# Early spread rows, states and y side by side, and one scan in place of two, in a Mamba-2 layer with a ternary feed-forward block

## The reference

```python
proj = rmsnorm(x) @ in_proj_w                  # z, x, B, C, dt: 2048+2048+512+512+32 columns
xBC  = silu(conv4(xBC) + conv_b)               # causal convolution of 4 taps, per channel
dt   = softplus(dt_raw + dt_bias); dA = exp(-dt * exp(A_log))
# per head (32 heads of 64 channels; 8 groups of B and C with 64 states each)
h_t  = dA_t * h_{t-1} + (dt_t * x_t) B_t^T     # 64 x 64 state
y_t  = h_t C_t + D * x_t
g    = y * silu(z);  g = g * rsqrt(mean(g^2 per group) + eps) * gate_norm_w
x    = x + (norm(x) + g @ out_proj_w)          # then the feed-forward block on the rows
```

## Time and profile before

| | |
|---|---|
| median of 3 runs | 1142.57 us (1141.39 to 1144.17) |
| the profiled execution: its own time, its span | 1145.73 us, 1143.9 us |
| DVE busy | 1059.9 us, 93% of the span |
| PE busy | 1033.2 us, 90% |
| ACT busy | 970.0 us, 85% |
| POOL busy | 868.6 us, 76% |
| granted PE clock, mean | 0.959 of full speed |
| from 260 to 860 us: idle of DVE in 120 us | about 1.1 us |
| DMA, mean | 20 GB/s |

### The profile page before, as it was taken

One profiled execution on the slowest core, in us unless ns is written; L12 is line 12 of the kernel. 1 busy time (PEld: TensorE's weight loads), 2 busy tenths in 40 slices (PEclk: granted clock), 3 DMA queues, 4 the chain that ended last, 5 costly groups with the idle time before them and its releaser, 6 DMA issues.

```text
span 1143.9 us, 26227 instructions
## 1 busy us (share of the span) xinstructions
PE 1033.2 (90%) x8912; PEld 732.0 (64%) x8912; DVE 1059.9 (93%) x2004; ACT 970.0 (85%) x2836; POOL 868.6 (76%) x596
## 2 busy tenths in 40 slices
PE   1724789999999999999999999999999999996797
PEld 1603566676666666676666666766666666664576
DVE  7597999999999999999999999999999999989474
ACT  2767898999999999999999999999999999984464
POOL 7300356888888888888888888888888888885765
PEclk9955899999999999999999999999999999997899
DMA  6320000000000000000000000000000000021001
GB/s 170 117 86 0 10 1 2 1 1 2 1 30 2 2 2 29 2 2 2 29 2 2 2 29 2 2 2 29 2 1 1 21 1 2 1 78 46 1 29 46
DMA packets 28084, 22.58 MB, mean 20 GB/s; under 512 B 11696, under 2 KB 22576, under 8 KB 27824
## 3 DMA queue, kind: packets, MB, share of 16 engines
q1 hardware_dynamic: 25136, 20.90, 5.9%
q10 hardware_dynamic: 2816, 0.02, 0.1%
HBM read 12.78 MB, written 8.13 MB: 18 GB/s over the span
## 4 chain that ended last, share of the span: by engine, by line
PE 77%; DVE 14%; issue 3%; POOL 2%; ACT 2%; DMA 0%; POOLq 0%; DVEq 0%; ACTq 0%
PE bank L1713 10%; PE bank L1695 10%; PE bank L1625 8%; PE bank L1727 8%; PE bank L1641 8%; PE bank L1626 6%; PE bank L1627 6%; PE bank L1681 5%; PE bank L1662 5%; DVE conv L1191 4%; PE bank L1766 3%; PE bank L1738 2%; DVE lm L1181 2%; PE bank L1555 1%; PE bank L1746 1%
## 5 line engine op out<-in xcount | busy, mean ns | idle before, releaser
L1191 DVE SCALAR_TENSOR_TENSOR conv<-bank,cw,conv 128x509 f32<-128x509 f32 (+2 forms) x576 | 421.7, 743 | 16.6 <-ACT conv L762 8.6
L636 POOL TENSOR_TENSOR lm<-lm,cbs 128x1024 f32<-128x1024 f32 x128 | 304.3, 2377 | 75.7 <-ACT xw L866 75.7
L1181 DVE TENSOR_TENSOR_SCAN lm<-bank,ident 128x512 f32<-128x512 f32 x256 | 298.7, 1210 | 0.7 <-PE bank L1641 0.6
L911 ACT ACTIVATE xdt<-bank,dt_all 128x64 f32<-128x64 f32 x1024 | 222.3, 329 | 37.2 <-PE bank L1662 37.2
L866 ACT ACTIVATE xw<-xdt,lm 128x64 f32<-128x64 f32 x768 | 199.3, 365 | 0.0
L644 POOL TENSOR_TENSOR ssum<-ssum,sq 128x512 f32<-128x512 f32 x96 | 123.1, 1283 | 93.0 <-ACT sq L926 92.8
L1625 PE MATMUL bank<-xn_hi,w_hi 128*128 128x512 f32 x320 | 166.1, 519 | 13.8 <-DVE conv L1191 13.1
L615 POOL TENSOR_TENSOR gated<-gated,gate 128x512 f32<-128x512 f32 x128 | 164.9, 1288 | 15.9 <-DVE gated L1238 14.5
L626 POOL TENSOR_TENSOR gated<-gated,rbs 128x512 f32<-128x512 f32 x120 | 153.8, 1282 | 0.0
L877 ACT ACTIVATE conv<-bank,cb_bias,cw 128x512 f32<-128x512 f32 x189 | 142.6, 781 | 11.5 <-PE bank L1627 7.3
L1713 PEld LDWEIGHTS bank<-lm,xdt 128*64 128x64 f32 x2048 | 110.3, 137 | 63.7 <-issue 63.7
(11 more groups left out here) (217 smaller groups left out, 1766.5 us busy)
## 6 DMA issues: line engine op xcount, KB each, us to landing
lm<-in_L_attn_in_proj_w SPq DMA_DIRECT2D x1, 2048.0 KB, 11.7
xn_scratch<-chan SPq DMA_DIRECT2D x4, 512.0 KB, 4.6
r_stage<-residual_scratch SPq DMA_DIRECT2D x8, 256.0 KB, 2.9
xn_stage<-xn_scratch SPq DMA_DIRECT2D x7, 256.0 KB, 3.2
x_scratch<-r_stage SPq DMA_DIRECT2D x7, 256.0 KB, 2.0
gate<-in_L_attn_hidden_states SPq DMA_DIRECT2D x2, 512.0 KB, 4.6
cdec<-in_L_attn_hidden_states SPq DMA_DIRECT2D x2, 512.0 KB, 7.1
w_out<-in_L_attn_out_proj_w SPq DMA_DIRECT2D x8, 128.0 KB, 3.3
```

Of the source, the lines that this page charges most:

```text
L636: gp.tensor_tensor(lm[:, mr, :, :], lm[:, mr, :, :], cbs[:, :, :], ALU.mult).then_inc(m_done, 1)
L911: act.activation(xdt[:, r, at:at + HP], misc_of("xt", n)[:, at:at + HP], ACT.Copy, scale=dt_h).then_inc(xdt_done, 1)
L1181: V.tensor_tensor_scan(lm[:, m % R, a, :], bc_bank[(3 * m + a) % 2][:, :], ident4[:, :], 0.0, ALU.mult, ALU.add).then_inc(scanned, 1)
L1191: V.scalar_tensor_tensor(out=conv[:, ci % 4, shift:S], in0=tile_bank(b, n, t)[:, 0:S - shift], scalar=cw[:, q, t, KW - 1 - shift:KW - shif ...
```

## The change

**Spread rows and scan.** The two spread banks become one PSUM tensor `decays` of 1,024 columns (bank 0 and bank 1). Row 0 of the next slot goes to bank 0 as soon as this slot's scan is done, row 2 and then row 1 share bank 1. One scan of 1,024 columns replaces two of 512; it waits for both rows, and row 1 waits for `cdec_done`.

**States and y.** On PE `states`, `y_within` and `y_states` stand next to each other (`inner`), behind `rows(ssd, 2)` and `rows(ahead, 0)`, and `rows(ahead, 1)` follows them. The variance moves to the end of the unit's first slot, and the second slot's first projection tile is made in the first slot (`next_tile`).

**State steps.** Step 0 goes from DVE to ACT (`first_state`). `pend` isn't copied per slot any more: 16 small matmuls and one DVE copy after slot 4 of batch 0 make it for all batches.

**ACT and POOL.** The weighing of a unit's second slot is done in its first (`weigh(1)`), before the cb copies; the first tap of the second slot's first tile too (`next_convolve`). The broadcast of the factor goes from ACT to POOL (`tensor_copy` behind `root`).

**Result rows.** `out_product` swaps its operands: `gated` is the stationary one, in four pieces of 128 tokens, `w_out` the moving one, so that the output comes out as rows. ACT's copy and PE's transposes fall away, and DVE adds the residual from `out_bank` in slot 14, where it was slot 15.

```diff
 # PE
 def spread(bb, m, k):
-    i = 3 * m + k
-    pm, pk = divmod(i - 2, 3)
-    if pk < 2:
-        after(pe, scanned, 2 * SLOTS, bb, 2 * pm + pk)
-    else:
-        after(pe, cdec_done, SLOTS, bb, pm)
+    if k == 1:
+        after(pe, cdec_done, SLOTS, bb, m - 1)
+    else:
+        after(pe, scanned, SLOTS, bb, m - 1 if k == 0 else m)
...
-    MM(bc_bank[i % 2][:, :], sel[:, m, first:first + P], ...)
+    MM(bc_bank[min(k, 1)][:, :], sel[:, m, first:first + P], ...)
 # out_product
-    last = MM(out_bank[:, :], w_out[:, m, :], gated[:, (m // R) % 2, m % R, :], start=(m == 0), stop=(m == SLOTS - 1))
+    for c in range(CH):
+        tok = slice(P * c, P * c + P)
+        last = MM(out_bank[:, tok], gated[:, (m // R) % 2, m % R, tok], w_out[:, m, :],
+                  start=(m == 0 and c == 0), stop=(m == SLOTS - 1 and c == CH - 1))
+def inner():
+    states()
+    y_within()
+    y_states()
 if r == 0:
     out_product()
     tiles()
-    variance()
-    states()
+    transposes()
     gate_tile()
-    transposes()
-    y_within()
     rows(ssd, 2)
     rows(ahead, 0)
-    y_states()
+    inner()
+    rows(ahead, 1)
     cb_products()
+    next_tile()
+    variance()
...
+# after slot 4 of batch 0
+for m in range(SLOTS):
+    last = MM(out_bank[:, NCH * m:NCH * m + NCH], sel[:, m, HP:HP + P], ends, start=True, stop=True)
 # DVE
-for a in range(2):
-    after(dve, bc_ready, 3 * SLOTS, bb, 3 * m + a)
-    V.tensor_tensor_scan(lm[:, m % R, a, :], bc_bank[(3 * m + a) % 2][:, :], ident4[:, :], 0.0, ...)
+after(dve, bc_ready, 3 * SLOTS, bb, 3 * m + 1)
+V.tensor_tensor_scan(lm[:, m % R, :, :].rearrange("p a s -> p (a s)"), decays[:, :], ident4[:, :], 0.0, ...)
 if r == 0:
-    taps(0, 1)
-    state_step(0)
-    taps(1, 2)
-    state_step(1)
-    taps(2, 3)
-    state_step(2)
+    taps(0, 3)
     chunk_ends()
+    state_step(1)
+    state_step(2)
...
 else:
-    state_step(0)
-    taps(0, 1)
+    taps(0, 2)
     chunk_ends()
-    taps(1, 2)
+    taps(2, 3)
     state_step(1)
-    taps(2, 3)
     state_step(2)
 # ACT
+def first_state():
+    after(act, s_ready, SLOTS, bb, m)
+    after(act, y_ready, SLOTS, bb, m - 2)
+    act.activation(hpk[:, m % 2, 0, :], misc_of("s", n)[:, 0:NS], ACT.Copy).then_inc(hfirst, 1)
 if r == 0:
     weigh()
     convolve()
     activate(0)
-    copy_variance()
     scale_x()
+    first_state()
     square()
     gate_silu()
+    weigh(1)
     copy_cb()
+    next_convolve()
+    copy_variance()
...
 # POOL, root
+after(gp, rstd_done, UNITS, bb, v)
+after(gp, rbc_ready, UNITS, bb, v - 1)
+gp.tensor_copy(rexp[:, :, :], rtok[:, :].unsqueeze(2).broadcast_to([P, 2 * CH, HP])).then_inc(rexp_done, 1)
```

More of the change, by code:

```diff
@@ L94, in following, with early_tile @@
     return None if isinstance(b, int) and b + 1 >= NB else b + 1
+def early_tile(b, n, t):
+    return n % R == 1 and t == PLAN[1][0] and (b, n) != (0, 1)
 def misc_plan():
@@ L234, in chan_of @@
             return 0 if t == 0 else 1 + (CONVS - 1) * (q % 2) + t - 1
-        bank = [pb(f"bank{i}", [P, S]) for i in range(8)]
+        low = [pb(f"bank{i}", [P, S]) for i in range(2)]
+        decays = pb("decays", [P, 2 * S])
+        bank = low + [decays[:, S * i:S * i + S] for i in range(2)] + [pb(f"bank{i}", [P, S]) for i in range(4, 8)]
         proj_bank, bc_bank, misc_bank, y_bank, out_bank = bank[0:2], bank[2:4], bank[4:6], bank[6], bank[7]
@@ L867, in weigh, with next_convolve @@
                                            scale=lm[:, mr, a, P * c + P - 1:P * c + P]).then_inc(xw_done, 1)
+                def first_state():
+                    if back(b, n, LAG_STATE) is None:
+                        return
+                    bb, m = back(b, n, LAG_STATE)
+                    after(act, s_ready, SLOTS, bb, m)
+                    after(act, y_ready, SLOTS, bb, m - 2)
+                    act.activation(hpk[:, m % 2, 0, :], misc_of("s", n)[:, 0:NS], ACT.Copy).then_inc(hfirst, 1)
+                def next_convolve():
+                    if real and early_tile(b, n + 1, PLAN[1][0]):
+                        begin(PLAN[1][0], n + 1)
                 def convolve():
@@ L994, in slot @@
                     activate(0)
+                    scale_x()
+                    first_state()
+                    square()
+                    gate_silu()
+                    weigh(1)
+                    copy_cb()
+                    next_convolve()
                     copy_variance()
+                elif r == 1:
+                    convolve()
+                    activate(0)
+                    first_state()
                     scale_x()
                     square()
-                    gate_silu()
-                    copy_cb()
-                elif r == 1:
-                    convolve()
-                    weigh()
-                    activate(0)
-                    if not (b == NB and n == 9):
-                        expand_root(b, n)
-                    scale_x()
-                    square()
-                    gate_silu()
                     copy_bt()
                     copy_factor()
+                    gate_silu()
                 elif r == 2:
@@ L1667, in tiles, with next_tile @@
                         for t in PLAN[r]:
-                            project(b, n, t, (b, n))
+                            if not early_tile(b, n, t):
+                                project(b, n, t, (b, n))
+                def next_tile():
+                    if real and early_tile(b, n + 1, PLAN[1][0]):
+                        project(b, n + 1, PLAN[1][0], (b, n + 1))
                 def states():
```

221 lines of the change are left out of this document (93 added, 128 removed).

## The result

The changed kernel takes 1170.15 us (median of 4 runs, 1167.38 to 1171.26) against 1142.44 for the kernel before on the same chip: ratio 1.0237, 95% interval 1.0214 to 1.0261. Predicted were 1128.0 us and a range of 1113 to 1149. The profiled execution took 1167.38 us, 21.7 more than that of before; of the 27.7 between the medians the other 6 lie in which executions were profiled.

The account below looks back on a forecast made before the run. DVE was taken as the bound: -0.80 us per unit plus 0.35 for stalls, x 30 = -13.5, and -1 at the ends, from 1145.73 to 1131.2; median 3.2 lower, 1128.0 us, range 1113 to 1149.

Parts of the forecast that it names:

- So DVE sets the beat: Middle stretch: DVE, busy 118.92 of 120 us, bounds the kernel at 28.92 us per unit, with PE close behind.
- DVE's terms: DVE per unit: copies -0.52 and -0.28, merged scan -0.24, waits on PE -0.48, dependent neighbours +0.72; sum -0.80 us.
- each of the six neighbours: DVE: six dependent neighbouring operations per unit, no longer separated by copies, cost 0.12 us each, +0.72 in all.
- PE's terms: PE per unit: output product +0.48, transposes some -0.1, grouping -1.4 us; need 27.9 to 29.3 us, lower half taken.
- rival 4: PE's output product: weight loads lie open, 2.9 us more per unit, +42 us, 1183 us in all; chance 0.03.
- 2 x 0.18: PE's half-array groups: two of three pairs of tile changes per slot vanish, 0.18 us each, -1.4 us per unit.
- That doesn't bind: Scan waiting for both spread rows: the loop takes 5.2 us with no waits, under the shortest slot's 6.0.
- 0.35 us per unit for such stalls: DVE waiting behind ACT's late first taps: charged at 0.35 us per unit, bounds 0 to 0.8.
- Rival 3: ACT's crowded first slot: stalls on the tap behind the cb copies cost 0.8 us per unit, 1141.5 us; chance 0.13.
- Rival 2: PE takes over in the middle, needing 29.3 us per unit because grouping saves nothing: +10, 1153 us; chance 0.12.
- Start and drain: Both ends: batch 0 at most 2.5 us more, drain up to 3.5 less, together -1 us.
- The drain's -3.5: Drain: the spread row comes ahead of y, and copy and transposes at the end go, up to 3.5 us less.

Follow-up runs that it names:

- e3: Kernel before, with the chunk-end products made once in an early table instead of a DVE copy per slot: 1145.20 us, ratio 1.0007, batch 115.50 us.
- e5: Kernel before, with the output product cut from 512 to 256 columns in 15 of 16 slots: 1131.06 us, ratio 0.9896, batch 113.53 us.
- e4: Kernel before, with only the output product's operands swapped so that result rows come out directly: 1144.43 us, ratio 1.0004, batch 115.36 us.
- e14: Kernel before, with only y within chunks moved behind the spread rows on PE, next to y from states: 1138.01 us, ratio 0.9940, batch 114.04 us.
- e2: Changed kernel, with the variance back ahead of the transposes in the first slot and its copy early on ACT: 1161.80 us, ratio 1.0154.
- e1: Changed kernel, with the pend copy one slot later and POOL's root back in a unit's first slot in the drain: 1163.59 us, ratio 1.0172.
- e9: Changed kernel with the edits of e1 and e2, and the second slot's first tile and tap ahead of cb products and copies: 1150.15 us, ratio 1.0042.

## Why the prediction was wrong

**"So DVE sets the beat": the step that failed.** I dismissed PE's 119.94 of 120 as modelled and took DVE's 118.92 as real, although 1.1 us idle in 120 is a sign of an engine that waits. e3 and e5 show the reverse. Everything priced on DVE was work on an engine with 2 us a batch to spare. By this alone the change should still have gained, since it relieves PE too.

**DVE's terms: right.** Scan 2.20 (2.18 predicted); dependent taps of 512 columns 0.78 apart against 0.66, dependent state steps 0.31 against 0.19, so 0.12 for each of the six neighbours per unit, as predicted. The Trainium skill says ("VectorE: DVE Perf Modes", section on the DRAIN) that a semaphore between two operations costs nothing extra, since the next one waits for an empty pipe anyway; these rows don't agree, by the 0.12.

**PE's terms: right in kind, two of them in size.** PE's own work fell from 115.43 to 112.94 us per batch, 0.62 per unit, where I took 1.0. The output product costs 0.03 us more per slot (e4), not 0.12; its loads don't lie open, as rival 4 would have it. By the price in the Trainium skill ("TensorE: Matmul & The Clock Gate", section on LDWEIGHTS) I had an estimate of 0.64 more per slot if nothing hid the loads, and no such cost shows. The two groupings save 0.24 us per slot (`states` with `y_within`) and 0.10 (`y_within` with `y_states`, as in e14), together 0.34 where I took 2 x 0.18: close, though the second alone is half of its price. What is missing from the 1.0 is mostly in the spread rows, whose own work grew from 10.65 to 12.84 us per batch, as more of them are followed by a wait.

**"That doesn't bind" and "0.35 us per unit for such stalls": the second failure, and the one that makes the sign.** I added up the ring with no waits in it (5.2 us) and walked ACT "from where PE delivers". But PE delivers the cb products only after DVE's state step, and stands still before that for the scan. Measured: PE's own work is down by 2.5 us a batch and the batch grew by 1.6, so PE stands idle 4.2 us a batch, 1.0 per unit instead of 0.35; on DVE 2.36 us a batch, 0.6 per unit, are idle behind ACT's first taps. Rival 3 had the mechanism (the cb copies ahead of the tap) and 0.13, with 0.8 for its price and 0.03 for a slower end, with no time beyond 1147. What neither had was the variance, 1.17 us a batch (e2), which I had moved at no cost and named no cover for.

**Rival 2** (PE takes over, slower) had the sign but not the cause: PE idles 4.9 us in 120 and its own work fell.

**Start and drain: "together -1".** The start is 2 us late, inside the bound of 2.5. The drain's -3.5 came from the spread row that now stands ahead of y; POOL's root, moved by a slot and put behind other work, was priced by its duration alone (1.0; the copy takes 0.61), never by who waits for it in the drain, where PE waits 8.91 and 4.08 us. The drain is 8 us the other way, and e1 gives 7.4 of them back.

## What to carry to other kernels

Two engines at 99% look alike; find the bound by taking work away from each in turn, and relieve only the one whose relief shortens the period. Less work on every engine is not a shorter period: e9 has 1.2 us less own work per batch on PE than e14 and 1.1 less on DVE, and its batch is 0.7 us longer. Work that stands between a step and the next one that waits for it covers the wait; when it is moved away, the wait lies open, here on both engines. So make such a change one move at a time, and measure each (e14 moves one call per slot). For every instruction that moves, follow who waits for it, in the drain as well as in the middle, and look at the granted clock before a gain or a loss in a drain is put down to the order.

## What the hardware showed that I had not expected

- Four stationary tiles with 128 columns each (f32) cost almost as little as one with 512: 0.90 us against 0.86 in front of the same row, 0.03 more per slot over the batch (e4).
- An idle stretch of the same 1.8 us in 6 let TensorE's granted clock stay at 1.00 in the kernel before and fall to 0.50 in e9; at 0.50 PE was busy all of 1096 to 1102 us.
- The drain's length follows that clock: over nine kernels with the changed kernel's order and its full output product, the stretch from the last skip product to the end is 75.3 to 75.6 us plus 1.4 to 9.3 of PE's loss at 0.50.
- A change of tile shape on TensorE costs about 0.15 us: 0.09 to 0.10 on the matmul in front of it, and 0.05 on the first pair of a half-array group behind it. Between 128*64 and 64*64 it costs the same as between whole and half (0.20 us for the last matmul of y in either case), between 128*64 and 128*64 nothing.
- On DVE a tap that depends on the one in front starts 0.78 us behind it, an independent one 0.66; for 64-column state steps it is 0.31 against 0.19.
